# Self attentions of a four-layer decoder: a tile's output product is issued one tile later

## The reference

```python
a = jnp.einsum('bqhd,bkhd->bhqk', q, k) / Dh ** 0.5
a = jnp.where(mask, a, NEG_INF)
a = jax.nn.softmax(a, axis=-1)
o = jnp.einsum('bhqk,bkhd->bqhd', a, v)
return jnp.einsum('blhe,hed->bld', o, Wout)
```

## Time and profile before

| | |
|---|---|
| median of three runs | 1983.77 us |
| the three runs | 1976.07, 1983.77, 1986.21 us |
| the profiled execution | 1979.5 us from its first to its last instruction (no other time is recorded for it) |
| TensorE busy | 1634.6 us, 83% |
| VectorE busy | 956.7 us, 48% |
| ScalarE busy | 748.1 us, 38% |
| the four stages in the span | about 304 to 404, 867 to 921, 1684 to 1743, 1768 to 1826 us |

### The profile page before, as it was taken

How to read it: one execution, slowest core, us unless ns; L and a number is a source line. 1 busy time by engine, 2 the same in 40 slices (tenths; PEclk the granted TensorE clock), 3 DMA queues, 4 the chain that set the end, 5 groups by cost and what they waited for, 6 DMA issues and landing times. The chain is left out here.

```text
span 1979.5 us, 53753 instructions
## 1 busy us (share of the span) xinstructions
PE 1634.6 (83%) x22089; PEld 1401.9 (71%) x22089; DVE 956.7 (48%) x2107; ACT 748.1 (38%) x1700; POOL 447.5 (23%) x627
## 2 busy tenths in 40 slices
PE   6999846769997899887699949997698988778695
PEld 5888645659995777675588848994686966666584
DVE  5565373241115888535512156664666744434313
ACT  3555372123342555432133326663124423333122
POOL 3443102012222434110244322220101200010242
PEclk8999855569998999876699979998898979776697
DMA  4111000049982211001599753331001163000596
GB/s 140 51 52 30 5 1 3 4 177 325 326 316 100 56 51 46 8 6 47 175 311 312 264 182 94 93 89 46 4 19 40 42 199 128 4 2 4 169 306 220
DMA packets 82023, 219.99 MB, mean 111 GB/s; under 512 B 19160, under 2 KB 35032, under 8 KB 74656
## 3 DMA queue, kind: packets, MB, share of 16 engines
q1 hardware_dynamic: 69888, 191.11, 29.6%
q0 software_dynamic: 8160, 22.29, 3.0%
q10 hardware_dynamic: 3776, 3.67, 0.6%
HBM read 201.62 MB, written 15.34 MB: 110 GB/s over the span
## 5 line engine op out<-in xcount | busy, mean ns | idle before, releaser
L2308 PEld LDWEIGHTS ps<-xt,w 128*128 128x128 f32 x1728 | 208.0, 196 | 36.1 <-issue 29.8
L2308 PE MATMUL ps<-xt,w 128*128 128x128 f32 x1728 | 215.9, 282 | 18.7 <-DMA w<-in_L_ffn_w 15.8
L2360 ACT ACTIVATE g<-ps,b 128x128 f32<-128x128 f32 x340 | 124.8, 367 | 247.7 <-PE ps L2308 226.3
L2318 PE MATMUL ps<-w,g 128*128 128x256 f32 x864 | 201.9, 381 | 0.6 <-DMA w<-in_L_ffn_w 0.6
L2318 PEld LDWEIGHTS ps<-w,g 128*128 128x128 f32 x864 | 158.8, 192 | 19.0 <-DMA w<-in_L_ffn_w 1.1
L2396 POOL DMA_INDIRECT x<-rows,token x85 | 83.1, 978 | 261.6 <-DVEq L2496 236.7
L2401 POOL DMA_INDIRECT results<-y,dest x85 | 83.6, 984 | 258.3 <-DVE y L2529 258.3
L2521 DVE COPY xt<-ps 128x256 f32<-128x256 f32 x85 | 36.1, 425 | 202.7 <-PE ps L2298 202.7
L2529 DVE COPY y<-ps 128x256 f32<-128x256 f32 x85 | 36.1, 425 | 162.6 <-PE ps L2318 162.6
L761 PE MATMUL ps<-c,w 128*128 128x258 f32 x512 | 97.2, 302 | 9.9 <-DVE pt L1068 5.9
L761 PEld LDWEIGHTS ps<-c,w 128*128 128x128 f32 x512 | 77.6, 196 | 23.7 <-issue 19.4
(11 more groups left out here) (447 smaller groups left out, 3660.7 us busy)
## 6 DMA issues: line engine op xcount, KB each, us to landing
w<-in_L_ffn_w SPq DMA_DIRECT2D x124, 512.0 KB, 5.0
w<-in_L_ffn_w SPq DMA_DIRECT2D x46, 1024.0 KB, 6.0
c<-in_ctx SPq DMA_DIRECT2D x96, 258.0 KB, 2.7
rows<-in_w_L_xattn SPq DMA_DIRECT2D x32, 192.0 KB, 2.6
rows<-in_w_L_xattn SPq DMA_DIRECT2D x8, 768.0 KB
c<-in_w_L_xattn SPq DMA_DIRECT2D x8, 514.0 KB
raw<-in_L_ffn_w SPq DMA_DIRECT2D x16, 256.0 KB, 2.8
tails<-in_w_L_xattn SPq DMA_DIRECT2D x5, 768.0 KB, 7.3
```

The costliest lines, as they stand in the source:

```text
L2308: mm = nc.tensor.matmul(hidden_bank(par, h), b.w1[:, par, c, h * P:(h + 1) * P], b.xt[:, par, c, :], start=c == 0, stop=c == DC - 1)
L2318: mm = nc.tensor.matmul(k.ps[:, YB + par, 0:D], b.g[:, par, h, :], b.w2[:, par, h, :], start=h == 0, stop=h == HC - 1)
L2360: nc.scalar.activation(b.g[:, par, h, :], hidden_bank(par, h), func, bias=b.b1[:, par, h:h + 1]).then_inc(s.g_ready, 1)
```

## The change

In TensorE's loop the output product of tile i-1, which stood last in the turn of tile i, is issued one turn later: as that of tile i-2, between `turn_probs(i)` and `scores(i + 1)`. VectorE's loop follows: the addition of tile i-2 stands ahead of `normalize_outputs(i)`, and `note` is one tile later too. No instruction is added or removed. Behind the loops the tail has the same output products in the same order, and one `note` more.

```diff
             for i in range(NT):
                 turn_probs(i)
+                if i > 1:
+                    output_product(i - 2)
                 if i + 1 < NT:
                     scores(i + 1)
                 if i > 0:
                     turn_outputs(i - 1)
                 probs_values(i)
-                if i > 0:
-                    output_product(i - 1)
+            output_product(NT - 2)
             turn_outputs(NT - 1)
             output_product(NT - 1)
...
             for i in range(NT):
                 if i + 1 < NT:
                     shift(i + 1)
+                if i > 1:
+                    add(i - 2)
                 normalize_outputs(i)
-                if i > 0:
-                    add(i - 1)
                 if i + 2 < NT:
                     spread_queries(i + 2)
-                if i > 1:
-                    note(i - 2)
+                if i > 2:
+                    note(i - 3)
+            add(NT - 2)
+            note(NT - 3)
             note(NT - 2)
             add(NT - 1)
             note(NT - 1)
```

## The result

The changed kernel's median is 1970.76 us over nine runs (1964.09 to 1977.45), against 1980.06 us for the kernel before, run beside it nine times (1969.25 to 1986.73). The ratio is 0.9954, with a 95% interval of 0.9934 to 0.9974. That is 9.1 us less, with an interval of 5 to 13 us. The prediction had said no change, 1983.9 us with a range from 1975 to 1993. Of the 13.1 us between 1983.9 and 1970.76, 3.7 us are the starting point: the kernel before has 1980.06 us over nine runs, where the prediction had the 1983.77 of three.

A forecast was written before the change was run, and what follows sets the result against it. The prediction took TensorE's list of work as the bound, so only waits gained or lost count. Terms 0.57 - 1.42 + 0.94 = +0.09 us on the median of 1983.77 gave about 1983.9 us, range 1975 to 1993.

The forecast's parts named there:

- The new waits for the exponential: Stages three and four: the turn now reaches three tiles before the exponential ends, waiting 0.35, 0.77 and 0.77 us, 1.89 together.
- The term of +0.57: What stays of the new exponential waits after "issue" gaps absorb the rest: 0.77 - 0.20 us in stage four; bounds 0 and +1.89.
- The wait for the copy of the turned probabilities: Each stage's last turn: the output product now covers waits of 0.25 and 0.46 us, twice each, saving 1.42 us.
- +0.94: Stage two's tail: one more note ahead of tile 6's addition costs 1.07 us on VectorE, 0.13 of it in a gap.
- about 0.5 us later against the stage's start: Sign expected in the changed trace: stage two's last addition would come this much later.
- VectorE's addition ahead of the normalisation: VectorE's loop: the moved 0.42 us addition doesn't wait and is covered, so it costs nothing; without cover 0.3 us a tile.
- have over 1 us to spare: Stage one's longer tiles, with three sets of scores, would have the exponential ready this early, so no new wait there.
- the prediction's model of blocks: TensorE's "issue" gaps are instruction delivery in blocks of 256, each no sooner than about 3.47 us after the last; waits can be absorbed.
- The clock's rise: Rival: a moved product lifts 13 lower-clock tiles of stages two and four, 14.8 us faster, 1969.0 us; chance 0.05.
- Bare waits: Rival: the gaps absorb none of the new exponential waits, so the sum is +1.41, 1985.2 us; chance 0.12.
- waits in every softmax tile: Rival: all 18 softmax tiles wait 0.77 us for the exponential, +13.4 us with the tails, 1997.2 us; chance 0.04.
- the clock's fall: Rival: new waits cost seven tiles of stages three and four the higher clock, 8 us, 1991.9 us; chance 0.06.

The follow-up runs named there:

- e4: The changed kernel, unchanged, profiled once more; its single run took 1967.24 us, stage one 89.99 us.
- e2: The kernel before with the change in stages two to four alone, stage one in the old order; 1975.82 us, ratio 0.9970.
- e8: The kernel before with the change in stages three and four alone; 1972.36 us against 1980.20, ratio 0.9972.
- e10: The kernel before with the change in stages one, three and four, stage two in the old order; 1970.57 us against 1979.81, ratio 0.9953.
- e5: The kernel before, but in stage one TensorE waits for the spread queries ahead of the turn of the probabilities; 1985.01 us against 1980.30, ratio 1.0011.
- e1: The kernel before with the change in stage one alone; 1973.75 us against 1980.30, ratio 0.9964.
- e9: The kernel before with one VectorE edit, the spread of the queries moved ahead of the addition; 1975.46 us against 1979.81, ratio 0.9984.
- e7: The changed kernel with the output product of tile i-2 moved behind the next scores; 1974.04 us against 1980.20 for the kernel before, ratio 0.9961.
- e13: The kernel before with VectorE's spread ahead of the addition and, in all stages, only tile 5's output product a turn later; 1967.83 us, ratio 0.9943.
- e14: The changed kernel with VectorE's spread moved ahead of the addition and the normalisation; 1972.51 us against 1980.94 for the kernel before, ratio 0.9943.
- the six: The six profiled executions whose stage one has the old order and the old spread; stage one 92.27 to 96.56 us, mean 94.8.

## Why the prediction was wrong

**What held.** The new waits for the exponential came, in part where the prediction put them. TensorE in stages three and four of the changed kernel (line 1496 is the turn):

```profile
1703.63 0.90 PE L1496 MATMUL ps<-consts_sb,p 128*128 128x128 f32 x3 [0.61 <-ACT p L1564]
...
1704.92 0.37 PE L1496 MATMUL ps<-consts_sb,p 128*128 128x128 f32 x1 [0.39 <-issue]
...
1710.37 1.05 PE L1496 MATMUL ps<-consts_sb,p 128*128 128x128 f32 x4 [0.61 <-ACT p L1564]
...
1773.64 0.66 PE L1496 MATMUL ps<-consts_sb,p 128*128 128x128 f32 x4 [0.38 <-ACT p L1564]
...
1798.59 0.66 PE L1496 MATMUL ps<-consts_sb,p 128*128 128x128 f32 x4 [0.61 <-ACT p L1564]
```

Four tiles wait, 0.38 to 0.61 us each (forecast: two to five tiles, at most 0.8). Two of the three forecast are among them, those about 34 us into stage three and 23 us into stage four; the third, 21 us into stage three, waits in e4, e2, e8 and e10 (0.24 to 0.55 us). These four executions have three or four such tiles each, 0.22 to 0.67 us. They are not in every softmax tile, so that rival is out. In stage three, at a clock of 0.69 both times, the waits together rose from 2.97 to 3.98 us and the "issue" gaps fell from 7.88 to 4.63, as if the gaps took them up. In stage four both rose, at another clock, so this is not shown in general. The term of +0.57 is too small to be seen in any ratio.

The wait for the copy of the turned probabilities is gone, as forecast: the last values product follows without a wait in stage one and in stage two (TensorE), against 0.25 and 0.46 in the earlier trace rows, and in stages three and four no such wait is left either:

```profile
385.80 1.37 PE L1505 MATMUL ps<-v,pt 32*32 32x17 f32 x128
...
899.11 0.58 PE L1505 MATMUL ps<-v,pt 32*32 32x17 f32 x47
```

The tail of stage two has the late addition that the prediction priced at +0.94 (VectorE from the last multiplication on, then TensorE's last product):

```profile
901.73 0.42 DVE L1637 TENSOR_TENSOR o<-ps,rsum 128x256 f32<-128x256 f32 x1
902.07 0.42 DVE L1651 BATCH_NORM_STATS2 stats_sb<-z_sb 128x6 f32<-128x256 f32 x1
...
903.14 0.41 DVE L1641 TENSOR_TENSOR z_sb<-z_sb,ps 128x256 f32<-128x256 f32 x1
...
905.62 0.42 DVE L1641 TENSOR_TENSOR z_sb<-z_sb,ps 128x256 f32<-128x256 f32 x1
...
903.70 1.10 PE L1521 MATMUL ps<-store_sb,ot 128*128 128x256 f32 x4 [1.05 <-DVE z_sb L1641]
```

From the end of the last multiplication to the last addition it is 905.62 - 902.15 = 3.47 us, before 920.54 - 917.93 = 2.61: 0.86 later, close to 0.94. TensorE's last product waits 1.05 us for the addition, where before it waited 0.46 for ScalarE's copy (in e4 it is 0.46 again, so this is not so in every execution). The sign itself, "about 0.5 us later against the stage's start", did not come: the last addition starts 49.82 us after the stage's start and not 53.67, because the whole stage was shorter at 0.72 than at 0.55. With that the prediction's third sign of being wrong, a granted clock that differs by more than 0.1 and a length that follows, came true in stage two.

**The step that failed** is "VectorE's addition ahead of the normalisation", priced at nothing, where the runs show about 5 us less. It asked what the addition, in its new place, holds up. It did not ask what the addition had held up in its old place. In stage one that was `spread_queries(i + 2)`, which the diff shows right behind it, and on which the next scores wait. The addition waited 1.27 us there for its product, and the spread behind it came too late for the scores, by 0.23 us with the turn of the probabilities in between and by 1.09 without it (e5). The earlier trace rows had the same wait, 1.26 us, at the stage's end, and I read it only as room for a note. The sentence on stage one, "have over 1 us to spare", was right for the exponential, the only releaser that I compared, and no row of stage one beyond its tail was read. The missed term is -6.3 us by the profiles of stage one, -4.9 of it at the same clock, and -7.1 us (-1.8 to -12.3) by e1's ratio: the largest part of the -9.1 measured. It is borne out by e9, which does only that move on VectorE and has a stage one of 88.03 us, by e7, e13 and e14, in which no spread stands behind a waiting addition either (85.28 to 91.02 us, against 92.27 to 96.56 for the six), and by e5, which shows the wait bare. By its ratio alone e9 does not exclude that there is no gain.

**Where the 6.3 us lie.** 1.3 us stand behind the last values product and go with the clock. 4.75 lie in the five stretches with a wait, where the wait itself is small (0.23 us) and the way from the 1568th matmul to the scores is 3.50 - 3.09 = 0.41 us shorter. The largest part, 1.9 us, is the gap at the 1695th matmul, which the prediction's model of blocks had no place for. In that model a block came 3.47 us or more after the one before, and a wait could only be absorbed by it. In stage one a wait went with a longer time: from edge to edge 6.84 to 7.39 us with a wait of 0.23 us, 5.13 to 5.41 without. The model fits rows 3 and is wrong as a general one. In the other stretches the gaps stay, and how 0.4 to 1.2 us were saved there is not taken apart. The Trainium skill, "Runtime: NRT & Kernel Launch", section "Instruction fetch mechanics", takes the fetch as hidden. If these gaps are the fetch, which no run shows, the trace disagrees with it.

**The rivals.** The clock's rise would have given 1969.0 us, near to the 1970.76 measured, but it is not what stage one shows: the six old executions have a mean granted clock of 0.57 there and the four new ones of 0.59, while e2 at 0.61 is still 92.27 us long and e4 at 0.58 is 89.99. In stage two the length goes with the clock, and there the change brings nothing. In stages three and four it may be part of what stays open. It is not out for the kernel as a whole either. Over the whole program the nine runs of the changed kernel have a granted clock of 0.874, and 112 runs of the kernel before beside the experiments 0.868; by a line through those 112 (an estimate) such a rise goes with 6.5 us. Whether the change raises the clock or merely met a higher one is not shown. e7 gained 7.8 us in the mean of its runs with no rise (0.867 both), and e9 3.8 us (0.868 both). Bare waits, waits in every softmax tile and the clock's fall were all on the slow side and none came.

## What to carry to other kernels

When an instruction moves in an engine's list, look at both places: what now stands behind it, and what no longer does. The second can be the larger, above all if the moved instruction waits for something. And an "issue" gap with a small time, the same in every turn, is worth a check against the ends on all other engines: 0.10 us behind one of them, in every turn, is a wait.

## What the runs showed that I had not expected

- **A short wait can go with a long gap.** 0.23 us of idle time ahead of the scores, 3.50 us after the 1568th matmul, goes with a gap of 1.5 to 2.1 us about a hundred matmuls later, in six executions of six. Where that wait is gone the gap is gone or 0.4 us at most (after, e4, e1, e10, e9, e13). In e14 the same pair is gone at a second place (0.34 and 1.19 us). At the four other waits of 0.23 us the next gap stays when the wait goes. In e7 a wait only 1.79 us after the 1568th matmul brings no gap at the 1695th, and one of 0.81 us elsewhere is followed by 2.53 us. In the six, and in e5 with its wait of 1.09 us, the matmul behind that gap starts 3.34 to 3.89 us after the wait ends, about the shortest spacing of two gaps (3.45 us). That is what one would see if the next block of instructions were asked for only when the wait ends. This is a reading and not shown: no run shows the fetch itself, and what makes the moment wrong is open.
- **Extra small matmuls cost more than their busy time.** 512 pairs cost stage one 11.2 us, of which 7.4 us are busy time, in one profile against the mean of six.
- **A stage's length goes roughly with its granted clock from one execution to the next.** Stage two, in the same order of instructions, took 53.15 us at 0.55 and 47.64 us at 0.82, but also 53.35 at 0.67. One profile of each kernel would have given stage two 4.2 us of gain; fourteen give none.
